# Attention halves in another order, with joined values and sums, and one chunk of probability sums moved from GpSimd to TensorE

## What is computed

```python
def lora_linear(x, W, b, Bm, Am):
    out = einsum('bld,od->blo', x, W) + b
    upd = einsum('blr,or->blo', einsum('bld,rd->blr', x, Bm), Am)
    return out + SCALING * upd
q, k, v = (split(lora_linear(x, W, b, Bm, Am)) ...)      # 16 heads of 32
scores = einsum('bhqd,bhkd->bhqk', q, k) * SCALE
attn = softmax(scores)                                    # over 1024 keys
out = einsum('bhqk,bhkd->bhqd', attn, v)
x = layernorm(x + lora_linear(out, Wo, bo, Bo, Ao))
x = layernorm(x + moe(x))      # 8 experts, top 1, capacity 256, and a shared expert
```

## Time and profile before

| | |
|---|---|
| median of 3 runs | 1078.03 us (1076.64 to 1080.87) |
| span of the profiled execution, first to last instruction | 1056.1 us |
| what the median has beside that span | 21.9 us |
| TensorE busy | 97% of the span |
| VectorE, ScalarE, GpSimd busy | 69%, 52%, 52% |
| halves 0 to 12, from the first score product of one to that of the next | 112.90 to 527.97 us |
| an even half (n = 6), an odd half (n = 7) | 29.88 us, 34.50 us |

### The profile page before, as it was taken

The page is one execution under the profiler, slowest core; times in us unless marked ns, Lnnn a source line. Parts: engine busy times, 40 slices in busy tenths (PEclk is TensorE's granted clock), DMA queues, the critical chain, the costliest instruction groups (busy, mean ns, idle before and its releaser), DMA issues.

```text
span 1056.1 us, 16138 instructions
## 1 busy us (share of the span) xinstructions
PE 1028.1 (97%) x5570; PEld 720.2 (68%) x5570; DVE 726.8 (69%) x1206; ACT 551.9 (52%) x970; POOL 545.2 (52%) x309
## 2 busy tenths in 40 slices
PE   5999999999999999999999999999999999999996
PEld 5877556465564655545545568788899999998884
DVE  4549877878788788887888568723666666663164
ACT  3321565656666566665665663512455666663116
POOL 2200688988888988889888863173000000004500
PEclk9999999999999999999999999999999999999998
DMA  8945441444316253241353456372477777775604
GB/s 266 321 127 154 111 100 51 103 109 120 101 51 156 56 134 86 60 121 32 90 180 110 140 160 199 92 212 60 111 213 222 213 228 222 233 211 109 96 1 159
DMA packets 162181, 145.74 MB, mean 138 GB/s; under 512 B 42481, under 2 KB 125681, under 8 KB 161856
## 3 DMA queue, kind: packets, MB, share of 16 engines
q1 hardware_dynamic: 154720, 128.62, 43.8%
q0 software_dynamic: 6656, 15.93, 5.4%
q10 hardware_dynamic: 736, 0.30, 0.1%
HBM read 84.70 MB, written 35.67 MB: 114 GB/s over the span
## 4 chain that ended last, share of the span: by engine, by line
PE 89%; DVE 4%; DMA 2%; ACT 2%; issue 1%; SPq 0%; ACTq 0%; DVEq 0%
PE bank L829 20%; PE bank L987 13%; PE bank L1000 12%; PE bank L935 12%; PE bank L1137 10%; PE bank L923 8%; PE bank L1045 4%; PE bank L895 3%; PE bank L1012 3%; PE bank L836 2%; DVE mx L1648 1%; DMA raw<-in_L_ffn_W_dram 1%; PE bank L1114 1%; DMA lora_c<-in_L_attn_Ao_dram 1%; PE bank L868 1%
## 5 line engine op out<-in xcount | busy, mean ns | idle before, releaser
L1377 ACT ACTIVATE prob<-bank 128x512 f32<-128x512 f32 x512 | 290.1, 597 | 188.0 <-PE bank L987 180.0
L1648 DVE TENSOR_REDUCE mx<-bank 128x1 f32<-128x512 f32 x512 | 325.0, 679 | 75.4 <-PE bank L935 72.3
L758 POOL TENSOR_TENSOR psum<-psum,prob 128x1024 f32<-128x1024 f32 x156 | 366.8, 2392 | 0.0
L987 PE MATMUL bank<-Qs,Ks 97*128 97x512 f32 x512 | 208.7, 423 | 0.9 <-DMA Qs<-mrow 0.9
L935 PE MATMUL bank<-Ks,Qs 96*128 96x512 f32 x512 | 184.6, 405 | 2.9 <-DVE mx L1648 1.3
L987 PEld LDWEIGHTS bank<-Qs,Ks 97*128 97x128 f32 x512 | 94.2, 188 | 106.2 <-ACT prob L1377 74.3
L1000 PE MATMUL bank<-prob,V 128*32 128x512 f32 x1024 | 131.4, 602 | 0.0
L935 PEld LDWEIGHTS bank<-Ks,Qs 96*128 96x128 f32 x512 | 97.0, 189 | 49.3 <-DVE mx L1648 21.9
L808 POOL DMA_DIRECT2D oe_d<-oe_sb x16 | 8.7, 546 | 228.6 <-ACT oe_sb L1514 227.6
L758 POOL TENSOR_TENSOR psum<-prob,prob 128x1024 f32<-128x1024 f32 x32 | 76.1, 2399 | 62.7 <-ACT prob L1377 33.6
L923 PE MATMUL bank<-xThi,Wsl 128*128 128x512 f32 x256 | 98.4, 396 | 0.8 <-DVE plane_klo L1638 0.8
(11 more groups left out here) (257 smaller groups left out, 2075.7 us busy)
## 6 DMA issues: line engine op xcount, KB each, us to landing
raw<-in_L_ffn_W_dram SPq DMA_DIRECT2D x120, 256.0 KB, 3.6
Ks<-plane_khi SPq DMA_DIRECT2D x64, 128.0 KB, 2.5
Qs<-plane_qhi SPq DMA_DIRECT2D x64, 128.0 KB, 2.3
raw<-in_L_ffn_sw_dram SPq DMA_DIRECT2D x30, 256.0 KB, 4.0
xin<-in_L_attn_x_dram SPq DMA_DIRECT2D x16, 256.0 KB, 5.8
v_d<-v_sb POOLq DMA_DIRECT2D x16, 256.0 KB, 3.6
Ks<-plane_klo SPq DMA_DIRECT2D x32, 128.0 KB, 2.6
Qs<-plane_qlo SPq DMA_DIRECT2D x32, 128.0 KB, 2.3
```

The source lines that it names most:

```text
L758: po.tensor_tensor(psum[:, pr], (prob[0] if kc == 1 else psum)[:, pr], prob[kc % RING][:, pr], ALU.add).then_inc(sem("sum_done"), 1)
L987: nc.tensor.matmul(score_at(v, i), Ks[v.b][0:97, hh, kc * P:(kc + 1) * P], Qs[v.b][0:97, hh, v.hf * HALF:(v.hf + 1) * HALF], start=True, s ...
L1377: ACTV(prob[kc % RING][:, hh, :], score_at(v, i), ACT.Exp, scale=SCALE).then_inc(sem("exp_done"), 1)
L1648: ins = RED(mx[(hf + ahead) % 2][:, 4 * hh + qt, part:part + 1], src, AX.X, ALU.max)
```

## The change

The strings `EVEN` and `ODD` are replaced. Blocks that stood alone or in twos now stand together, with nothing between them, and the letters between them move. `SUMS` is 6 where it was 7 for halves 0 to 11, so that GpSimd makes 10 additions there and not 12, and TensorE two late sums and not one (two letters l in each string). The strings of the last three halves are only broken into other lines, with the same words.

```diff
-EVEN = ("mmm vle imm m p m p m mopmmp m "
-        "mmq v mm m v - imm im v - "
-        "mvr mi mm m v m mn v m mm "
-        "hv mmz")
-ODD = ("m vm m lom m mv mm m em mm "
-       "pi pmm p mmm i qpm mvvv - mmm p "
-       "ip m mppm rqvvimn p m p mh mm v "
-       "mp mzqp")
+EVEN = ("mm m p m mm m p m "
+        "mm ollevm mi p m ip mqmim - "
+        "vvv m mm m ivv rm m m "
+        "m mm - mhnm zvv m mm m")
+ODD = ("pmm m p mmm - pmm - mpmm "
+        "- vollevq m mm p im p m "
+        "mpm miim pqm - vvv mm mp - "
+        "mpm - mrp - mmm pin mm qhvvvz")
...
-SUMS = [7] * (HALVES - 3) + [6, 7, 6]
+SUMS = [6] * (HALVES - 4) + [7, 6, 7, 6]
```

More of the change, by code:

```diff
@@ L95 @@
 LAST_EARLY = 11
-EVEN = ("mmm vle imm m p m p m mopmmp m "
-        "mmq v mm m v - imm im v - "
-        "mvr mi mm m v m mn v m mm "
-        "hv mmz")
-ODD = ("m vm m lom m mv mm m em mm "
-       "pi pmm p mmm i qpm mvvv - mmm p "
-       "ip m mppm rqvvimn p m p mh mm v "
-       "mp mzqp")
[L104 to L115, removed]
+EVEN = ("mm m p m mm m p m "
[3 rows of a table added]
+ODD = ("pmm m p mmm - pmm - mpmm "
+        "- vollevq m mm p im p m "
+        "mpm miim pqm - vvv mm mp - "
+        "mpm - mrp - mmm pin mm qhvvvz")
+LAST_FIRST = ("m vmo m ml m mmv m mm "
[3 rows of a table added]
+LAST_EVEN = ("m vl mm mlm mm om e mm "
[3 rows of a table added]
+LAST_ODD = ("- - - - - vle - pi "
[3 rows of a table added]
 HALVES = 4 * NG
 ZERO_HALVES = (2, 6)
-SUMS = [7] * (HALVES - 3) + [6, 7, 6]
+SUMS = [6] * (HALVES - 4) + [7, 6, 7, 6]
 def adds(n):
```

## The result

The changed kernel takes 1094.51 us (median of 4 runs, 1092.78 to 1095.09) beside 1078.18 us: 1.0145 of the time before, 95% interval 1.0131 to 1.0159, or 16.3 us slower. Slower was forecast, with 1085.2 and a range to 1091; the time lies above the range.

What follows compares the result with a forecast made beforehand. TensorE, busy in 97% of the span, was taken as the bound. The pairs' changes, with 5.2 us gained and late-queue waits, summed to +7.2: span 1056.1 to 1063.3, plus 21.9 beside it, 1085.2 us; range 1075 to 1091.

Steps and rivals of the forecast that it cites:

- The prices on TensorE: In TensorE's stream: a full-size product costs 0.233 us, a block behind a block 0.87, each run of blocks 0.3 more.
- The odd half: TensorE's sum for an odd half: 33.8 us without waits, plus 0.25 for the copy and 0.1 for odds and ends.
- the wait for the copy: Word 9 of the odd half: the last v waits for ScalarE's take_ov, 0 to 0.5 us, taken as 0.25.
- The even half: TensorE's sum for an even half: 28.5 to 28.6 us without waits, 29 to 29.7 expected in the profile.
- the first sum: TensorE's gain before any wait: 0.33 us in each of twelve halves plus 1.2 in half 0, together 5.2.
- The queue: SyncE's stacks land late for the odd half's fifth m: 2.0 us behind r, 4.0 where weights load; chance 0.62.
- The clock: Third rival: waits of 3 to 4 us drop TensorE to half clock, giving 1090 to 1096 us; chance 0.08.
- The sum: All pairs of halves 0 to 13 together: +7.2 us, with the gain of 5.2 in it.
- GpSimd: Twelve halves lose two additions of 2.36 us each, 57 us of GpSimd, costed at nothing for the kernel's time.
- The 21.9 us beside the span: Time that the median was taken to have beside the profiled span, added to the span to forecast the time.
- the second rival: Queue late only behind weights: +2.3 twice, +0.5 for the first pair, -0.7 for four others; 1080.5 us, chance 0.14.
- the first pair: Halves 0 and 1: 62.9 us forecast against 62.34 before, entered as +0.5.

Runs made afterwards that it cites:

- e5: Kernel before with SUMS of 6 and a second l beside the first in each string, so added blocks in the old order: 1068.60 us, ratio 1.0106.
- e7: Changed kernel with SyncE stacking pair 1's keys right behind pair 0's in every even half, half 0 too: 1054.08 us, ratio 0.9968.
- e8: Changed kernel with one l less per string, SUMS of 7 and pair 1's keys stacked early in every even half: 1062.63 us beside 1078.74, ratio 0.9848.
- e0: Kernel before, unedited, profiled once more: 1057.41 us.
- e4: Changed kernel, unedited, run again beside the kernel before on one chip: 1072.52 us, ratio 1.0146.
- e2: Kernel before with pair 1's keys stacked right behind pair 0's, except in half 0: 1058.37 us, ratio 1.0000.
- e1: Changed kernel with pair 1's keys stacked right behind pair 0's, except in half 0: 1059.98 us, ratio 1.0021.
- e3: Changed kernel with ten overwritten products just before the fifth m's wait in halves 1, 5 and 9: 1071.75 us, ratio 1.0128.
- e6: Changed kernel with one l less in each string and SUMS of 7, so the new order alone: 1059.56 us, ratio 1.0028.

## Why the prediction was right in its sign and wrong in its size

- **The prices on TensorE** (0.233, 0.87, 0.3) held. In the changed kernel's half 6 the two l start at 319.59, e at 321.33 and v at 322.19, 0.87 a block, and e5 weighed the added block at 0.87 and 0.85.
- **The odd half** without a late queue was summed at 33.8 + 0.25 + 0.1 and measures 34.2 (e7): the wait for the copy is 0.29, inside its 0 to 0.5.
- **The even half** was summed at 28.6 and up to 1 us of waits, 29 to 29.7 with those. It measures 29.9: 1.3 us of waits, for VectorE's bank and ScalarE's exponentials in words 21 to 31 (words 21 to 27 hold eight m and not the seven that the forecast counted). In the changed kernel what of this stood between r and the fifth m cost nothing, since the wait for the queue was longer. With the queue in time it shows: halves 2, 4, 6, 8 and 10 of e7 are as long as before, in spite of the joined blocks. So e7 gains 3.2 us on the kernel before (4.5 in halves 0 to 12 of its profile) and not the 5.2 of the first sum.
- **The queue** is the cause, as forecast. Pair 0's queries went out 15.6 us into the half (15.7 was forecast), the maxima in half 4 at 23.4 (23.4), the last stack of half 8 at 33.1 (33.5), of half 4 at 34.1, 0.6 later than forecast through pauses in the issue (268.87 to 276.94 above). Removing its lateness, e7 against the profile of the changed kernel, takes 429.7 - 410.8 = 18.9 us from halves 0 to 12, the slow clocks included. Which of the moves made it late isn't taken apart by a run: r stands 21.8 us into half 6 where it stood 20.6, q went from word 10 to 14, and the fifth m from word 4 to 3, and none of the three was put back alone.
- **The clock** is the step that failed. The forecast had it as a rival with 0.08 and let the sum run at full clock. In the profile it was at half for 3.4, 6.8 and 3.4 us in halves 1, 5 and 9. What runs at half clock loses half of it, 6.5 us without the part that fell into a wait. The sum was 7.2; with 6.5 it is 13.7, and 14.6 were measured in halves 0 to 12. Pair by pair, less the clock: 0/1 +1.1 (0.5 was forecast), 2/3 +0.7 (1.8), 4/5 +2.9 (2.3), 6/7 +1.0 (0.4), 8/9 +2.1 (2.3), 10/11 +1.2 (0.4), 12/13 -0.5 (-0.5). That the rest of the sum came so near is in part luck: 2/3 was 1.1 too high, and 0/1, 4/5, 6/7 and 10/11 together 2.6 too low. The price that I gave this rival, 1.8 to 3.5 each time, was about right (1.6 to 3.3 us, worked out as above); its chance was wrong. I had set against it "that VectorE's and ScalarE's waits are filled in", which is no reason: TensorE idled 2.2 to 3.2 us at a stretch, and rows 11 had shown that some 3 us are enough. For the clock, TensorE: Matmul & The Clock Gate of the Trainium skill says in "Why this matters for your kernels" that a pause between bursts of products drops it. These runs agree: halves 1, 5 and 9 of the changed kernel have 0.91 to 0.96 behind such a pause, and its other halves 1.00. But most of the pauses here are shorter than the one that this section of the Trainium skill names, and there the measurement decides.
- **GpSimd** was rightly costed at nothing, and that made the second part of the change a pure loss: twelve blocks of 0.87, 10.4 us, as the halves of e5 have it. The 5.2 gained had hidden it by netting it with 15.6 for the runs saved; e8, which keeps the runs and leaves out the added blocks, gains 16.
- **The 21.9 us beside the span** were not around it, as e0 shows. That had no part in the difference, which lies in halves 0 to 12: 14.6 of 16.3 us, and in e4 15.9 by the profiles beside 15.3 by the times.
- **Small slips in the sums**: the second rival's terms add up to 1080.3 and not 1080.5, and the first pair's 62.9 against 62.34 is +0.6. Neither has a part in the outcome.

The change is slower by 1.45% because it moved r and q later, and the maxima that need their transfers earlier, on a queue with 1.3 us to spare; because most of the longer waits cost the clock as well; and because it gave TensorE, the bound, 10.4 us of work that GpSimd had done under cover. What is good in it, the joined blocks, gives 16 us once the two others are undone (e8); the early keys alone give nothing (e2).

## What to carry to other kernels

When letters move in a schedule written by hand, follow each one's transfers to their consumer: count what the issuing queue does between producer and consumer, at its own rate, and compare it with the stretch of the bound engine between the same two points. If a wait on TensorE comes out at 2 us or more, add the stretch at half clock behind it to the price (here 1.6 to 3.3 us behind ten such waits of eleven), as a term and not as a rival. Joining narrow products into runs saves the way in and out; moving work to the bound engine from one that is hidden costs its full price, so price the two parts apart.

## What the runs showed of the hardware that was not expected

With an idle wait of TensorE of 2.1 to 3.4 us the half clock came, at the wait's end or up to 1.1 us behind it, in halves 1, 5 and 9 of both profiles of the changed kernel, for 3.4 or 6.8 us; waits of 1.1 us in halves 3 and 7, and of 1.3 and 1.5 in half 11, were not. Over the five profiles in which a fifth m waited for 0.5 us or more (the two of the changed kernel, e1, e3, e6) it came with ten waits of 2.1 us or more out of eleven, and two out of fifteen of 0.5 to 1.8. So length alone doesn't settle it: 2.1 us in half 9 of e6 did not drop the clock, and 1.5 in half 11 of e3 did. In half 0 of e2 and e5 it fell 2.4 us into the half, behind a wait of 0.94 us that all profiles have there and that the other ten got through at full clock.

Ten throwaway products in front of the wait kept the clock in three halves of three (e3).

SyncE issues the stacks every 0.63 us, with a longer step now and then, of 1.5 us in half 5 of the changed kernel's profile and of 2.0 in half 7 of e3. So in the changed kernel's profile the last stack was issued 34.1 us behind the start of half 4 and 33.1 behind that of half 8, behind the same transfers. The last stack landed 2.3 to 2.7 us behind its issue, but 4.2 us once in e3 and 4.5 once in e1.

The part behind the routing takes some 20 us more on some chips, in either kernel.
